# Second layer of a four-layer graph network: turning the rows by copies in SBUF and a block transpose instead of on the tensor engine, with reordered handovers

## The chip, the cores and the metric

One NeuronCore of a Trainium2 chip. The metric is the device time of one execution in microseconds. Three runs of the kernel before gave 2652.57, 2657.73 and 2658.16 us, so the median is 2657.73 us. Engine names are those of the profile: PE is TensorE, PEld its weight load, DVE is VectorE, ACT is ScalarE, POOL is GpSimd, SP is SyncE, which only issues DMAs here.

## What is computed

128 graphs of 64 nodes with 384 features pass four graph layers; each is followed by a residual sum and a layer norm. The change is in the second (`L1_gnn`), which itself has two turns with weights of their own:

```python
temper = float(np.sqrt(H))
adj = adjacency_matrix
adj_tri = jnp.triu(adj, k=1)
diag_mask = jnp.triu(adj, k=0) - adj_tri
h = hidden_state
for l in range(L):                       # L = 2
    m_left = jnp.einsum('bsh,oh->bso', h, W_left[l])
    m_right = jnp.einsum('bsh,oh->bso', h, W_right[l])
    u_left = jnp.einsum('bih,bjh->bij', h, m_left) / temper
    u_right = jnp.einsum('bih,bjh->bij', h, m_right) / temper
    u = u_left * adj_tri + u_left * diag_mask + u_right * jnp.swapaxes(adj_tri, 1, 2)
    delta_exp_u = jnp.exp(u) * adj
    attention = delta_exp_u / (jnp.sum(delta_exp_u, axis=2, keepdims=True) + 1e-10)
    h_lin = jnp.einsum('bsh,oh->bso', h, W_lin[l]) + b_lin[l]
    ctx = jnp.matmul(attention, h_lin)
    h = jax.nn.relu(_layer_norm(ctx, ln_a[l], ln_b[l]))
# around it: x = _layernorm(x + h)
```

## The kernel before

The rows (graph, node) are cut into 16 groups of 512. Three programs follow one another on the same engines: `first_pass` (the first layer, until about 800 us), `rows_pass` (the second, until about 1575 us) and `heads_pass` (third and fourth). They hand over through Python generators: at each `next(after)` of one program, the following one puts a stretch of its own instructions into that engine's queue. The order of every queue is thus written out by hand. All waits are on semaphores, and each engine works its queue strictly in order.

`rows_pass` has 32 slots, four for each of 8 pairs of groups (a, b). Slot 0 is the first turn of group a, slot 1 the first turn of b, slot 2 the second turn of a and slot 3 the second turn of b. A slot on PE is: `projections` (54 matmuls, left and right), `values` 0 and 1, on slots 1 and 2 the 12 `transposes` for the next slot, `pair_scores`, `values` 2 and 3, `context`. A product is made of three of fp32r parts, so the input of a slot is needed with features on the partitions, as a high part (`hhi`, DVE `high_parts`) and a low part (`hlo`, POOL `low_parts`).

How this input comes about differs by turn. In the first turn (`from_x(n)`, slots 0 and 1) SP loads the rows in four strips of 32 features blocks (`load_strips`, tile `blocks`), and DVE turns them by one block transpose (`rows_turned`). In the second turn (slots 2 and 3) ACT writes the normalised context of the slot two before into `z` (`apply`, semaphore `z0_done`), POOL applies gain and shift in eight operations (`z_done`), PE transposes (`t_done`), ACT takes the rectified result out of PSUM into `hf` (`chunks`, `f_done`), and DVE and POOL split it.

DVE's order in a slot: (next slot from strips: `rows_turned`, `high_parts`), `final_sum` and `final_stats` of a finished group, `values_out` 0 and 1 (PE's `values` 2 waits for the first), `final_shift`, (next slot turned: `high_parts`), `one_side` (the masked scores, for which ACT's exponential waits), `values_out` 2, `deltas` (`l_dt`, for which `context` waits), `values_out` 3, `normalise`. ACT's order: `projections_out` 0 and 1, `apply` of the slot before, `projections_out` 2 to 5, `chunks`, `final_apply`, the exponential, `context_out`.

Of the kernel before, what the change touches and what calls it, by code (L numbers as in the profile page):

```python
# [9 lines left out]
ALU = mybir.AluOpType  # L10
# [74 lines left out]
def rows_pass(nc, sh, ctx, groups, first_weight, x_in, strips_in, x_out, adj_d, adjt_d, vec_d):  # L85
# [27 lines left out]
    def entered(n):  # L113

        return 2 * (n // 4) + min(n % 4, 1) + 1
# [32 lines left out]
    x1, x2 = sb("x1", [P, T, D]), sb("x2", [P, T, D])  # L148
# [20 lines left out]
    faggr = sb("faggr", [P, T, 2])  # L169
    sh.rows_stop_at = nc.sbuf_base  # L170
# [17 lines left out]
    t_done = sem("t_done")  # L188
# [33 lines left out]
    def sync_program(sync, after):  # L222
# [22 lines left out]

        first = rows.first
# [24 lines left out]
        sync.wait_ge(first.stored[0], 32)  # L271
        for half in range(2):
            load_x(2, half)
        sync.wait_ge(first.z_done, T * groups)
        load_vectors(1)
        yield
        load_weights(sh, sync, 11, 15)

        for n in range(4 * iters):
            for m, g, half in halves(n):  # L280
                if g + XBUFS < groups:
                    sync.wait_ge(x_used if half else x_half, g + 1)
                    load_x(g + XBUFS, half)
            for g in finished(n):
                store(g)
# [8 lines left out]
            if n + 3 >= 4 * iters and n % 2:  # L294
                next(after)
# [4 lines left out]
    def tensor_program(pe, after):  # L300
        def transposes(n):
            pe.wait_ge(z_done, T * (n - 1))
            for c in range(KC):
                pe.wait_ge(ml_evac, 2 * KC * (n - 1) + (5, 6, 3)[c])
                for t in range(T):
                    mm = nc.tensor.transpose(ring[c][:, t * P:(t + 1) * P], z[n % 2][:, t, c * P:(c + 1) * P],
                                             sh.ident[:, :])
                mm.then_inc(t_done, 1)

# [15 lines left out]
        def projections(n, w0):  # L325
            pe.wait_ge(hi_done, KC * (n + 1))
            for k in range(2 * KC):
# [3 lines left out]
                elif k == 3:  # L331
                    pe.wait_ge(c_evac, T * n)
                elif n and from_x(n):
                    pe.wait_ge(ml_evac, 2 * KC * (n - 1) + (5, 6, 3)[k])
# [8 lines left out]
        def pair_scores(n):  # L343
# [3 lines left out]
            for t in range(T):  # L347
                for c in range(KC):
                    for b in range(2):
                        for half in range(2):  # L350
                            g, first = 2 * t + b, S * b + Q * half
                            keys = blocks[n % 2][:, 2 * g + half, c, :] if from_x(n) else \
                                hf[n % 2][:, c, g * S + Q * half:g * S + Q * half + Q]
                            mm = nc.tensor.matmul(  # L354
                                scores[first:first + Q, t * P + Q * half:t * P + Q * half + 3 * Q],
                                keys,
# [17 lines left out]
        for n in range(4 * iters):  # L374
# [8 lines left out]
            if not last:  # L383
                if not from_x(n + 1):
                    transposes(n + 1)
            else:
# [7 lines left out]
    def scalar_program(act, after):  # L394
        def chunks(n):
            for c in range(KC):
                act.wait_ge(t_done, KC * turned(n) + c + 1)
                act.wait_ge(u_done, max(n - 1, 0))
                act.wait_ge(lo_done, max(KC * (n - 2) + c + 1, 0))
                nc.scalar.activation(hf[n % 2][:, c, :], ring[c][:, :], ACT.Relu)\  # L400
                    .then_inc(f_done, 1)
# [15 lines left out]
        def apply(n):  # L417
            a = n % 2
            act.wait_ge(ab_done, n + 1)
            if n % 4 < 2:  # L420
                act.wait_ge(stored[a], 16 * (n // 4))
            for t in range(T):
# [15 lines left out]
        for n in range(4 * iters):  # L438
            if n:
# [17 lines left out]
        for g in finished(4 * iters - 1):  # L457
            final_apply(g)
# [5 lines left out]
    def vector_program(dve, after):  # L464
# [5 lines left out]
        def rows_turned(n):  # L470
            dve.wait_ge(strips_loaded[n % 2], 16 * STRIPS * (n // 4 + 1))
            nc.vector.transpose(blocks[n % 2][:, :, :, :], blocks[n % 2][:, :, :, :]).then_inc(xt_done, 1)

        def high_parts(n):
            for c in range(KC):
                dve.wait_ge(v_done, max(NPROJ * (n - 1), 0))
                if from_x(n):
                    dve.wait_ge(xt_done, entered(n))
                    nc.vector.tensor_copy(hhi[n % 2][:, c, :].rearrange("p (b r) -> p b r", r=SQ),
                                          blocks[n % 2][:, :, c, :]).then_inc(hi_done, 1)  # L480
                else:
                    dve.wait_ge(f_done, KC * turned(n) + c + 1)
                    nc.vector.tensor_copy(hhi[n % 2][:, c, :], hf[n % 2][:, c, :]).then_inc(hi_done, 1)
# [43 lines left out]
        def final_sum(n, g, half):  # L527
            a = g % 2
            dve.wait_ge(x_loaded[g % XBUFS], 32 * (g // XBUFS) + 16 * (half + 1))
            for t in range(2 * half, 2 * half + 2):  # L530
                dve.wait_ge(z_done, T * n + t + 1)
# [29 lines left out]
        dve.wait_ge(cleared, 2)  # L561
        dve.wait_ge(vec_in[0], 16 * nvec)
        for n in range(4 * iters):
# [9 lines left out]
            for g in finished(n):  # L573
                final_stats(g)
            values_out(n, l, range(0, 2))
# [20 lines left out]
    def gpsimd_program(pool):  # L596
# [3 lines left out]
        def low_parts(n):  # L600
            for c in range(KC):
                pool.wait_ge(hi_done, KC * n + c + 1)
                pool.wait_ge(v_done, max(NPROJ * (n - 1), 0))
                if from_x(n):
                    upper, lower = (part[n % 2][:, c, :].rearrange("p (b r) -> p b r", r=SQ) for part in (hhi, hlo))
                    nc.gpsimd.tensor_tensor(lower, blocks[n % 2][:, :, c, :], upper, ALU.subtract).then_inc(lo_done, 1)
                else:
                    nc.gpsimd.tensor_tensor(hlo[n % 2][:, c, :], hf[n % 2][:, c, :], hhi[n % 2][:, c, :],
                                            ALU.subtract).then_inc(lo_done, 1)
# [19 lines left out]
        yield  # L629
        pool.wait_ge(vec_in[0], 16 * nvec)  # L630
        for n in range(4 * iters):
# [3 lines left out]
            masks(n)  # L635
# [3 lines left out]
            if n + 1 < 4 * iters:  # L639
# [3 lines left out]
            for t in range(T):  # L643
# [10 lines left out]
def first_pass(nc, sh, ctx, groups, xt_in, x_in, x_out, adjt_d, vec_d, row_d, col_d):  # L654
# [49 lines left out]
    rowvec = [sb("rowvec0", [P, D])]  # L704
    sb = placed(sh.at_x0)
# [26 lines left out]
    x_loaded = sem("x_loaded")  # L732
    adj_loaded = [sem(f"adj_loaded{a}") for a in "ab"]
# [35 lines left out]
    first.u_done, first.lo_done = u_done, lo_done  # L769
    first.c_done, first.c_evac, first.z_done, first.stored = c_done, c_evac, z_done, stored  # L770

    def sync_program(sync, after):
# [56 lines left out]
        store(groups - 3)  # L829
        next(after)  # L830
        sync.wait_ge(x_used, groups - 1)
# [1254 lines left out]
```

## Time and profile before

| | us |
|---|---|
| median of 3 runs | 2657.73 |
| the profiled execution | 2652.64 |
| its span, first to last instruction | 2650.9 |
| PE busy in the span | 2570.5 |
| DVE busy | 1998.3 |
| POOL busy | 1521.1 |
| ACT busy | 1219.6 |

The profiled execution is 1.7 us longer than its span. A row of the timeline reads: start, duration, engine, line, operation, output<-input, shape, how many merged, and in brackets the idle time before it with what ended it. A row of a waiting engine at a place is of use only together with what that engine does before and after it, since the queues are in order. The granted clock is 1.00 at TensorE's upper level (2.4 GHz) and 0.50 at the lower (1.2 GHz).

### The profile page before, as it was taken

How to read it: one execution, taken by the hardware profiler on the slowest of the kernel's cores; microseconds unless marked ns; L12 is line 12 of the kernel's file. 1: busy time of each engine (PE TensorE's matmuls, PEld its weight loads, DVE VectorE, ACT ScalarE, POOL GpSimd, SP SyncE). 2: the span in 40 equal slices, each digit the busy share in tenths (PEclk: the TensorE clock that was granted, in tenths of full speed). 3: DMA queues.
4: the chain of work that ended last, by engine and by line, in shares of the span. 5: the costliest groups of instructions: out<-in, count | busy, mean ns of one | idle time of the engine just before them, and what ended most of it. 6: DMA issues, size and time to landing. Idle time of an engine off the chain costs nothing.

```text
span 2650.9 us, 59174 instructions
## 1 busy us (share of the span) xinstructions
PE 2570.5 (97%) x23040; PEld 2237.4 (84%) x23040; DVE 1998.3 (75%) x4485; ACT 1219.6 (46%) x2385; POOL 1521.1 (57%) x1380
## 2 busy tenths in 40 slices
PE   8999999999997999999999997999999999999997
PEld 7998998998986788888888876888888888888886
DVE  5788888888886657666756757888888877777775
ACT  2344444344343344344444443554555555556554
POOL 7657656756757666666667654443444345555553
PEclk9999999999998999999999998999999999999998
DMA  5112112111125122122221224222233223323432
GB/s 162 33 42 70 56 43 69 56 54 58 52 73 155 43 67 73 48 63 67 67 60 53 59 56 108 63 59 71 77 77 77 69 59 87 92 77 89 102 77 75
DMA packets 253286, 187.99 MB, mean 71 GB/s; under 512 B 175568, under 2 KB 250960, under 8 KB 253008
## 3 DMA queue, kind: packets, MB, share of 16 engines
q1 hardware_dynamic: 253008, 184.21, 25.5%
q8 instruction: 184, 3.01, 0.5%
q14 instruction: 94, 0.77, 0.1%
HBM read 133.84 MB, written 50.33 MB: 69 GB/s over the span
## 4 chain that ended last, share of the span: by engine, by line
PE 85%; DVE 5%; POOL 4%; issue 3%; ACT 2%; DMA 1%; SPq 1%; POOLq 0%; ACTq 0%; DVEq 0%
PE bank L1413 14%; PE bank L864 11%; PE bank L1421 11%; PE bank L339 11%; PE pair L864 11%; PE bank L1473 4%; PE pair L1442 4%; PE bank L1459 3%; PE bank L321 2%; PE pair L321 2%; PE bank L850 2%; PE bank L888 2%; PE pair L888 2%; PE bank L354 1%; PE bank L369 1%
## 5 line engine op out<-in xcount | busy, mean ns | idle before, releaser
L1854 POOL TENSOR_TENSOR h_logits<-h_logits,h_mx 128x512 f32<-128x512 f32 x192 | 202.0, 1053 | 267.7 <-DVE h_mx L1697 267.7
L1709 DVE TENSOR_TENSOR h_val<-bank,h_rowvec 64x192 f32<-64x192 f32 x512 | 181.7, 355 | 33.3 <-PE bank L1421 24.2
L407 ACT ACTIVATE l_sides<-bank 128x512 f32<-128x512 f32 x192 | 114.2, 595 | 193.4 <-PE bank L339 193.4
L1150 POOL TENSOR_TENSOR l_hlo<-l_hf,l_hhi 128x576 fp32r<-128x576 f32 x96 | 134.7, 1432 | 115.2 <-ACT l_hhi L981 115.2
L1413 PE MATMUL bank<-h_hhia,whi 128*128 128x512 f32 x450 | 185.3, 412 | 3.3 <-DVE h_hloa L1680 2.3
L1413 PE MATMUL bank<-h_hhia,wlo 128*128 128x512 f32 x450 | 176.7, 393 | 0.0
L1573 ACT ACTIVATE h_keys<-bank,h_keycol,h_halves 128x512 f32<-128x512 f32 x192 | 138.8, 775 | 81.1 <-PE bank L1413 81.1
L1057 DVE TENSOR_TENSOR l_val<-bank,l_vec 64x384 f32<-64x384 f32 x256 | 142.3, 556 | 40.4 <-PE bank L864 37.4
L1057 DVE TENSOR_TENSOR l_val<-pair,l_vec 64x384 f32<-64x384 f32 x256 | 142.3, 556 | 32.1 <-PE pair L864 28.3
L1189 POOL TENSOR_TENSOR l_vdiag<-l_vdiag,l_vec 128x384 f32<-128x384 f32 x128 | 127.6, 1016 | 66.1 <-ACT l_vdiag L962 66.0
L864 PE MATMUL bank<-whi,l_hhi 128*128 128x384 f32 x576 | 141.4, 353 | 5.8 <-POOL wlo L74 5.8
L1597 ACT ACTIVATE h_probt<-bank 128x384 f32<-128x384 f32 x256 | 111.5, 490 | 68.7 <-PE bank L1459 68.6
L981 ACT ACTIVATE l_hhi<-l_hf 128x576 fp32r<-128x576 f32 x96 | 58.6, 673 | 162.4 <-PE pair L864 159.4
L1697 DVE TENSOR_REDUCE h_mx<-h_logits 128x8 f32<-128x512 f32 x192 | 130.8, 681 | 3.3
L642 POOL TENSOR_TENSOR l_small<-l_small,power 128x4 f32<-128x4 f32 x32 | 32.4, 1012 | 174.0 <-DVE l_small L519 174.0
L864 PE MATMUL pair<-whi,l_hhi 128*128 128x384 f32 x576 | 130.8, 334 | 1.5 <-DVE l_val L1057 1.5
L864 PE MATMUL bank<-wlo,l_hhi 128*128 128x384 f32 x576 | 131.6, 336 | 0.0
L864 PE MATMUL bank<-whi,l_hlo 128*128 128x384 f32 x576 | 131.3, 335 | 0.0
L864 PE MATMUL pair<-whi,l_hlo 128*128 128x384 f32 x576 | 131.0, 334 | 0.0
L864 PE MATMUL pair<-wlo,l_hhi 128*128 128x384 f32 x576 | 130.7, 334 | 0.0
L864 PEld LDWEIGHTS bank<-whi,l_hhi 128*128 128x128 f32 x576 | 97.6, 189 | 30.7 <-issue 18.6
L1442 PE MATMUL pair<-h_keys,h_q 64*64 64x128 f32 x3072 | 107.7, 278 | 14.4 <-DVE h_logits L1689 14.4
(267 smaller groups left out, 7699.4 us busy)
## 6 DMA issues: line engine op xcount, KB each, us to landing
h_strips<-x SPq DMA_DIRECT2D x128, 192.0 KB, 5.1
l_hf<-xt SPq DMA_DIRECT2D x16, 864.0 KB, 4.6
l_x<-x SPq DMA_DIRECT2D x16, 768.0 KB, 4.5
l_x<-x SPq DMA_DIRECT2D x32, 384.0 KB, 3.2
h_za<-x SPq DMA_DIRECT2D x16, 768.0 KB, 4.9
h_zb<-x SPq DMA_DIRECT2D x16, 768.0 KB, 5.0
x<-l_zfa SPq DMA_DIRECT2D x8, 768.0 KB, 3.5
x<-l_zfb SPq DMA_DIRECT2D x8, 768.0 KB, 4.3
```

What stands on the lines that cost most here:

```text
L339: mm = nc.tensor.matmul(ring[k % RING][:, :], ww[:, c, m * P:(m + 1) * P], hh[:, c, :], start=(j == 0), stop=(j == len(terms) - 1))
L864: mm = nc.tensor.matmul(ring[k % RING][:, 0:D], hh[:, c, first:first + P], ww[:, c, :], start=(j == 0), stop=(j == len(terms) - 1))
L1057: ins = nc.vector.tensor_tensor(val[half, (g + b) % GRAPHS, 0:D], ring[k % RING][half, 0:D], bias[half, :], ALU.add)
L1150: nc.gpsimd.tensor_tensor(hlo[:, c, :], hf[:, c, :], hhi[:, c, :], ALU.subtract).then_inc(lo_done, 1)
L1189: nc.gpsimd.tensor_tensor(vdiag[:, t, 0:D], vdiag[:, t, 0:D], vec[n % 4 // 2][1][:, :], ALU.add)\
L1413: mm = nc.tensor.matmul(ring[k % 2][:, :], ww[:, c, m * P:(m + 1) * P], hh, start=(c == 0 and j == 0), stop=(c == KC - 1 and j == 2))
L1421: mm = nc.tensor.matmul(out, lhs, rhs, start=(j == 0), stop=(j == len(terms) - 1))
L1442: mm = nc.tensor.matmul(scores[out, 2 * r:2 * r + 2, t, :], q[heads, c, g * S:(g + 1) * S], keys[heads, c, g, :, :], start=True, stop=True)
L1573: ins = nc.scalar.activation(keys[:, c, :, h, :], ring[1][:, :].rearrange("p (g j) -> p g j", j=S), ACT.Identity, scale=halves[:, h:h + 1] ...
L1697: nc.vector.tensor_reduce(mx[:, c, :, ts], row, AX.X, ALU.max)\
L1709: ins = nc.vector.tensor_tensor(val[S * p:S * p + S, 2 * t + b, :, p, 0:HD], src[rows, :, p, :], bias[rows, :, p, :], ALU.add)
L1854: nc.gpsimd.tensor_tensor(row, row, mx[:, c, :, ts].unsqueeze(3).broadcast_to([P, HP, 2, S]), ALU.subtract).then_inc(sub_done, 1)
```

## The change

In the second turn the rows no longer go through PE. `turn_strips` on SP copies `z` within SBUF into the strip layout of `blocks` with 16 DMAs (4 strips by 4 blocks of 32 partitions, 128 pieces of 384 bytes each); DVE turns them with the block transpose; ACT applies gain, shift and rectifier in place, now with features on the partitions and the two vectors as columns (`colvec`). POOL's gain and shift stay only for the second turn's results. PE's transposes are gone. `final_apply` moves behind `context_out`. At the handover from the first layer, DVE turns and splits slot 1's rows and takes the values of slot 0 out before it finishes the last two groups; the last group's residual has a buffer of its own (`last_x`). At the handover to the third layer, the second set of strips is loaded before masks, vectors and weights, and group 14 is stored after those. Weights and vectors are permuted on input to fit. The core of the diff:

```diff
+        def turn_strips(n):
+            sync.wait_ge(z0_done, T * (n - 1))
+            sync.wait_ge(u_done, n - 1)
+            sync.wait_ge(lo_done, KC * (n - 1))
+            by_tile = blocks[n % 2][:, :, :, :].rearrange("p (t q) c a -> p t q (c a)", t=T)
+            for j in range(STRIPS):
+                for q in range(P // SQ):
+                    sync.dma_start(by_tile[SQ * j:SQ * j + SQ, :, q, :],
+                                   z[n % 2][SQ * q:SQ * q + SQ, :, RUN * j:RUN * j + RUN])\
+                        .then_inc(strips_loaded[n % 2], 16)
...
         for n in range(4 * iters):
+            if n and n + 1 < 4 * iters and not from_x(n + 1):
+                turn_strips(n + 1)
             for m, g, half in halves(n):
...
+            if n + 1 == 4 * iters:
+                next(after)
             for g in finished(n):
                 store(g)
...
-            if not last:
-                if not from_x(n + 1):
-                    transposes(n + 1)
...
         def chunks(n):
+            act.wait_ge(col_in, 32)
+            act.wait_ge(xt_done, n + 1)
             for c in range(KC):
-                act.wait_ge(t_done, KC * turned(n) + c + 1)
-                act.wait_ge(u_done, max(n - 1, 0))
-                act.wait_ge(lo_done, max(KC * (n - 2) + c + 1, 0))
-                nc.scalar.activation(hf[n % 2][:, c, :], ring[c][:, :], ACT.Relu)\
+                part = blocks[n % 2][:, :, c, :]
+                nc.scalar.activation(part, part, ACT.Relu, scale=colvec[:, 0, c:c + 1], bias=colvec[:, 1, c:c + 1])\
                     .then_inc(f_done, 1)
...
-                for g in finished(n):
-                    final_apply(g)
...
             context_out(n)
-        for g in finished(4 * iters - 1):
-            final_apply(g)
+            for g in finished(n):
+                final_apply(g)
...
+        rows_turned(1)
+        high_parts(1)
+        split_weights(sh, dve, "hi", *weights_of_slot(0, 0))
+        yield
         dve.wait_ge(vec_in[0], 16 * nvec)
-        for n in range(4 * iters):
+        values_out(0, 0, range(0, 2))
+        yield
+        one_side(0)
+        values_out(0, 0, [2])
+        deltas(0)
+        values_out(0, 0, [3])
+        yield
+        normalise(0)
+        for n in range(1, 4 * iters):
...
             for g in finished(n):
                 final_stats(g)
+            if n + 1 < 4 * iters and not from_x(n + 1):
+                rows_turned(n + 1)
             values_out(n, l, range(0, 2))
...
-            for t in range(T):
+            for t in range(T if n % 4 >= 2 else 0):
                 pool.wait_ge(z0_done, T * n + t + 1)
...
         variance(passes - 1)
         scale_shift(passes - 1)
-        for g in range(groups - 2, groups):
-            final_sum(g, 0)
-            final_sum(g, 1)
-            final_variance(g)
-            final_shift(g)
+        final_sum(groups - 2, 0)
+        final_sum(groups - 2, 1)
+        final_variance(groups - 2)
+        next(after)
+        final_shift(groups - 2)
+        next(after)
+        final_sum(groups - 1, 0)
+        next(after)
+        final_sum(groups - 1, 1)
+        final_variance(groups - 1)
+        final_shift(groups - 1)
...
         load_strips(0)
         yield
+        sync.wait_ge(rows.v_done, T * last_rows)
+        sync.wait_ge(rows.stored[1], 16)
+        sync.wait_ge(xt_done, 1)
+        load_strips(1)
         sync.wait_ge(rows.d_done, last_rows)
```

## Rows read from the trace of the kernel before

**Rows 1.** The page: PE's busy time, the chain by engine.
```profile
PE 2570.5 (97%) x23040; PEld 2237.4 (84%) x23040; DVE 1998.3 (75%) x4485; ACT 1219.6 (46%) x2385; POOL 1521.1 (57%) x1380
PE 85%; DVE 5%; POOL 4%; issue 3%; ACT 2%; DMA 1%; SPq 1%; POOLq 0%; ACTq 0%; DVEq 0%
```

**Rows 2.** Timeline of PE, slots 1, 2, 3 of a middle iteration.
```profile
start us, us, engine line op out<-in xcount [idle before <-releaser]
1219.91 0.53 PE L369 MATMUL bank<-l_val,l_dt 64*64 64x385 f32 x1 [0.93 <-DVE l_dt L505]
...
1221.37 0.96 PE L339 MATMUL bank<-l_hhib,whi 128*128 128x512 f32 x3
...
1236.89 1.47 PE L306 MATMUL bank<-ident,l_za 128*128 128x128 f32 x12
1238.30 2.19 PE L354 MATMUL bank<-l_sides,l_blocksb 128*32 128x96 f32 x96
...
1243.97 0.53 PE L369 MATMUL bank<-l_val,l_dt 64*64 64x385 f32 x1 [0.16 <-DVE l_dt L505]
...
1245.42 0.96 PE L339 MATMUL bank<-l_hhia,whi 128*128 128x512 f32 x3
...
1269.34 0.96 PE L339 MATMUL bank<-l_hhib,whi 128*128 128x512 f32 x3
...
1291.93 0.96 PE L339 MATMUL bank<-l_hhia,whi 128*128 128x512 f32 x3
```

**Rows 3.** Timeline of ACT, slot 1: apply, final_apply, exponential.
```profile
1226.55 2.51 ACT L423 ACTIVATE l_za<-l_craw,l_small 128x384 f32<-128x384 f32 x4 [0.16 <-DVE l_small L525]
...
1238.97 2.51 ACT L429 ACTIVATE l_zb<-l_zb,l_small 128x384 f32<-128x384 f32 x4
```

**Rows 4.** Timeline of DVE: values_out 0, high_parts, and a block transpose.
```profile
1235.53 0.56 DVE L489 TENSOR_TENSOR l_val<-bank,l_vec 128x384 f32<-128x384 f32 x1 [2.30 <-PE bank L321]
...
1238.85 2.19 DVE L483 CAST l_hhia<-l_hfa 128x512 fp32r<-128x512 f32 x3
...
1276.30 1.78 DVE L472 STREAM_TRANSPOSE l_blocksa<-l_blocksa 128x1536 f32<-128x1536 f32 x1 [1.88 <-DMA l_blocksa<-x]
```

**Rows 5.** Timeline of SP's DMA issues: four strips, half a residual.
```profile
1292.77 2.12 SPq L243 DMA_DIRECT2D l_blocksb<-x  x4
1306.15 0.38 SPq L225 DMA_DIRECT2D l_x<-x  x1
```

**Rows 6.** Adjacency issues by source line; DMA view, median from issue to landing.
```profile
L231 SPq DMA_DIRECT2D l_adjna<-adj x32: 616/617/1356, 799.2 to 1505.1; - x32
...
x<-l_za SPq DMA_DIRECT2D x8, 768.0 KB, 3.7
...
l_adjtb<-adjt SPq DMA_DIRECT2D x32, 64.0 KB, 2.3
```

**Rows 7.** First iteration: PE idle in its slot 1, granted clock behind it.
```profile
861.25 0.53 PE L369 MATMUL bank<-l_val,l_dt 64*64 64x385 f32 x1 [3.24 <-DVE l_dt L505]
...
862.70:866.40 3.70, 3.70 (x13) 2.90 (x10) 3.06 (x13) 1.14 (x3) 0.37 (x1) 0.55 0.34 74
```

**Rows 8.** Handover from the first layer: timelines of DVE and PE.
```profile
810.10 0.50 DVE L1094 TENSOR_SCALAR l_small<-l_faggr 128x4 f32<-128x4 f32 x1
815.46 0.16 DVE L1098 SCALAR_TENSOR_TENSOR l_small<-l_faggr,l_small 128x4 f32<-128x4 f32 x1 [4.85 <-POOL l_small L1194]
...
828.73 1.30 PE L321 MATMUL bank<-whi,l_hhia 128*128 128x384 f32 x3 [12.67 <-DVE l_val L489]
```

**Rows 9.** Handover to the third layer: timelines of SP, DVE and PE.
```profile
1573.71 1.77 DVE L1674 STREAM_TRANSPOSE h_xta<-h_strips 128x1536 f32<-128x1536 f32 x1
...
1587.09 0.29 DVE L1779 MEMSET h_val<- 64x48 f32 x2
1587.80 4.72 SPq L1347 DMA_DIRECT2D h_strips<-x  x4
...
1598.93 1.78 DVE L1674 STREAM_TRANSPOSE h_xtb<-h_strips 128x1536 f32<-128x1536 f32 x1 [11.55 <-issue]
...
1605.58 1.99 PE L1442 MATMUL pair<-h_keys,h_q 64*64 64x128 f32 x32 [10.09 <-DVE h_logits L1689]
```

More of the change, by code:

```diff
@@ L111, in finished, with pieces @@
         return [g for m, g, half in halves(n) if half]
-    def entered(n):
-        return 2 * (n // 4) + min(n % 4, 1) + 1
+    def pieces(n):
+        return 4 * STRIPS * (n // 4 + (not from_x(n))) + STRIPS * (n // 4 + 1)
     def turned(n):
@@ L271, in sync_program @@
         sync.wait_ge(first.stored[0], 32)
+        sync.wait_ge(first.x_used, groups)
         for half in range(2):
@@ L275, in sync_program @@
         load_vectors(1)
+        for k in range(2):
+            sync.dma_start(colvec[:, k, :], col_d[k], allow_slow_non_contiguous=True).then_inc(col_in, 16)
         yield
@@ L293, in sync_program @@
                     load_strips(n + 2)
-            if n + 3 >= 4 * iters and n % 2:
+            if n + 3 == 4 * iters:
                 next(after)
@@ L382, in tensor_program @@
             values(n, SLOT[w0 + 2], range(0, 2))
-            if not last:
-                if not from_x(n + 1):
-                    transposes(n + 1)
-            else:
+            if last:
                 for c in range(KC):
@@ L421, in apply @@
                 act.wait_ge(stored[a], 16 * (n // 4))
+            else:
+                act.wait_ge(xt_done, n + 1)
             for t in range(T):
@@ L603, in low_parts @@
                 pool.wait_ge(v_done, max(NPROJ * (n - 1), 0))
[L604 to L609, printed above, removed]
+                upper, lower = (part[n % 2][:, c, :].rearrange("p (b r) -> p b r", r=SQ) for part in (hhi, hlo))
+                nc.gpsimd.tensor_tensor(lower, blocks[n % 2][:, :, c, :], upper, ALU.subtract).then_inc(lo_done, 1)
         def side(out, adjacency, k):
@@ L629, in gpsimd_program @@
         yield
+        masks(0)
+        low_parts(1)
+        yield
         pool.wait_ge(vec_in[0], 16 * nvec)
@@ L634, in gpsimd_program @@
                 pool.wait_ge(vec_in[1], 16 * nvec)
-            masks(n)
+            if n:
+                masks(n)
             for g in finished(n):
@@ L1220, in gpsimd_program @@
         final_power(groups - 2)
+        next(after)
         final_power(groups - 1)
@@ L1374, in sync_program @@
         load_weights(sh, sync, 15, 17)
-        sync.wait_ge(rows.v_done, T * last_rows)
-        sync.wait_ge(rows.stored[1], 16)
-        sync.wait_ge(xt_done, 1)
-        load_strips(1)
         load_adj(1)
@@ L2061, in arrays @@
         if name.startswith("L1_gnn_W"):
-            turn = v[0][strip_order()]
-            v = np.stack([turn if name.endswith("lin") else turn[:, strip_order()], v[1]])
+            v = v[:, strip_order()]
+            v = np.ascontiguousarray(v if name.endswith("lin") else v[:, :, strip_order()])
         out[name] = v.reshape(1) if v.ndim == 0 else v
@@ L2066, in arrays @@
     out["xt"] = np.ascontiguousarray(np.concatenate([xt, xt[..., 0:S]], -1))
+    for m in ("ln_a", "ln_b"):
+        out[f"turned_{m}"] = np.ascontiguousarray(out[f"L1_gnn_{m}"][0][strip_order()])
     out["adjt"] = np.ascontiguousarray(np.swapaxes(out["adj"], 1, 2))
```

59 lines of the change are left out of this document (31 added, 28 removed).

## The prediction, made before the changed kernel was run

> **What bounds the kernel now.** I read the page first. PE is busy 97% of the span and makes 85% of the chain that ended last [rows 1], so only what shortens PE's queue, or what makes PE wait, moves the time. Next I read the timeline of PE over one middle iteration of the second layer, because an average says nothing about a single slot. From one projection start to the next, slot 1 takes 24.05 us (1221.37 to 1245.42), slot 2 takes 23.92 and slot 3, which has no transposes, 22.59 [rows 2]. PE waits 0.93 us for `l_dt` at the end of slot 0 and 0.16 us at the end of slot 1. So in the middle of the layer PE is the bound, and DVE's delivery of `l_dt` comes nearly last. Third, the timelines of the two handovers: there PE waits, 12.67 us for DVE's `values_out` [rows 8] and 10.09 us for DVE's first logits [rows 9].
>
> **What leaves PE.** Twelve transposes per turned slot, from 1236.89 to 1238.30, are 1.41 us [rows 2]; 16 turned slots make 22.6 us. All of it is on the path today. It is a gain only if the new way delivers in time, so the rest of the working is about that.
>
> **When the new way delivers.** I count from the start S of slot 1 or 2. Its steps:
> 1. `apply` of the slot before ends at 1229.06, S+7.7 [rows 3]. SP's wait ends there.
> 2. SP issues 16 DMAs. No SBUF-to-SBUF DMA is in the trace. The nearest issue is that of the strips, also 384-byte pieces onto 32 partitions: four in 2.12 us, 0.53 each [rows 5]. From below, a residual load costs 0.38 [rows 5]; from above, an adjacency load 0.62 [rows 6]. I take 0.53, and the last issue then starts 15 x 0.53 = 8.0 us after the first. The ends are 5.7 and 9.3.
> 3. The last one lands. The smallest frequent DMA, 64 KB, takes a median of 2.3 us from issue [rows 6]; these carry 48 KB. I take 2.3 and allow 0.5 either way. The landing L in slot 2 is thus S + 7.7 + 0.1 + 8.0 + 2.3 = S+18.1.
> 4. DVE's block transpose takes 1.78 us [rows 4]. It stands ahead of `values_out` 0 in DVE's queue, which takes 0.56 [rows 4] and for which PE's `values` 2 waits. PE resumes at L+2.4 or so. Without the transposes PE has finished the scores at S + (1238.30 - 1221.37 - 1.41) + 2.1 = S+17.6.
> 5. Behind it stand `values_out` 1, then `high_parts`. ACT's three affine operations run beside them, the same in number as the evacuations they replace. From the start of `high_parts` to `context` the trace shows 1238.85 to 1243.97, 5.1 us, with nothing waiting in between; from `context` to the next projection 1.45 us [rows 2, 4]. `high_parts` starts at L+3.0, `context` at L+8.1, and the next slot at L+9.6.
>
> The cycle of slot 2 becomes 18.1 + 9.6 = 27.7 us against 23.92, 3.8 us more.
>
> In slot 1, `apply` writes a `z` tile that must be stored first. The store now waits for `final_apply` behind `context_out` of slot 0, which ends at about S+1.1: plus 2.51 [rows 3] and a store of 3.7 us [rows 6], `apply` starts near S+7.5 and ends at S+10.0. Then L is S+20.4 and the cycle 30.0 us against 24.05, 6.0 us more. SP's other waits in these slots (masks, store) are over by S+6.7 and hide nothing else: the residual loads pushed behind the turn have three buffers.
>
> The DMA page of the Trainium skill (DMA: Bandwidth & Descriptors, section Anatomy of one DMA) puts one DMA at about 2.0 us fixed plus its bytes at 436 GB/s. By it, 48 KB would land 2.1 us after issue instead of 2.3; over 16 turns that is an estimated 3 us less, which does not change the verdict.
>
> **What PE's clock adds.** After an idle time of 3.24 us in the first iteration the granted clock is 0.55 over the next 3.7 us, mostly the 1.2 GHz level [rows 7]. The new idle time ahead of `values` 2 is L + 2.4 - 17.6, so 2.9 us in slot 2 and 5.2 in slot 1. PE has 2.4 us of slack between `values` 3 and `context`, since DVE's chain is later, and most of a slow stretch falls there. I take 0.5 us per slot, with bounds of 0 and 2.
>
> **The rest of the slots.** In slot 0 the exponential no longer stands behind `final_apply`; the 0.93 us wait for `l_dt` shrinks by about 0.7, eight times, 5.6 us. POOL's eight gain and shift operations in slots 1 and 2 cost nothing today and their removal gives nothing, because they end ahead of the transposes. Masks and low parts have more room.
>
> **Handovers.** From the first layer: DVE is through with group 14's variance at 810.6 [rows 8]. Then come the transpose (1.78) and three copies (2.19) [rows 4], stretched by POOL's work beside them, and a weight split, some 7.5 us together; `final_shift`, which POOL releases at 815.46 [rows 8], is covered by them. So `values_out` 0 ends near 818.7, and today PE resumes behind it at 828.73. PE resumes 10 us earlier. But group 15's store now ends later than the first context (an estimate: its second half is summed behind `values_out` 3 near 825, then statistics, POOL's power, 2.51 us of `final_apply` and 3.7 us of store, so 835). Slot 1's `apply` waits for it and ends near 837.7, and the turn waits for `apply`. By the steps above (10.4 to the landing, 9.6 behind it) slot 2 starts at 857.7 instead of 861.25 + 1.45 = 862.7 [rows 7]. Slot 2 then costs some 2 us less than today, as today's has an idle time like the one of [rows 7] as well. Of the 10 us, 7 stay for the whole first iteration.
>
> To the third layer: DVE waits until 1598.93 for strips issued at 1587.80, behind ten other DMAs; it was free at 1587.4 [rows 9]. The first strips are turned by 1573.71 + 1.77 = 1575.5 [rows 9]; issued then, the second ones have landed when DVE is free. DVE and PE's first logits come 11 us earlier. I take 11, with 8 and 20 (if the slow clock behind the idle time goes too) as bounds.
>
> **The sum.** Seven iterations of 6.0 + 3.8 = 9.8 are 68.6; the clock 14 x 0.5 = 7.0; slot 0 gives back 5.6, the first iteration 7, the last handover 11. Together +52 us on the profiled execution's 2652.6, so 2705. The median run is 5 us above that execution and I put the forecast at 2707.
>
> **Rivals.** (a) *The turn is hidden.* If the 16 DMAs are issued and landed by about S+14, DVE's transpose waits for nothing and each turned slot takes 22.6 us. Then the whole 22.6 us comes back, slot 0 gives 5.6, and the handovers 10 + 11: about 2603. It decides at 6.5 us from `apply` to landing; against it stands that even issues of 0.38 us make 5.7 + 2.3 + 0.1 = 8.1, and slot 1 has 2.3 us more to lose. I give everything faster than before 12%. (b) *Short issues.* At 0.38 us the turn is 2.3 us shorter in each of 14 slots: 2675. (c) *Long issues and a slow clock.* At 0.62 us and 2 us of clock per slot: 14 x (1.3 + 1.5) = 39 more, 2746; if the DMAs also back up in the rings, as the four strips of 4.72 us do [rows 9], over 2780. (d) *The turn only breaks even* with shorter issues and a larger handover gain: 2650 to 2662.
>
> **How the numbers follow.** My case (2685 to 2730) has 45%, (b) 17%, (c) 20%, (d) 6%, (a) and what lies near it 12%. The range is 2660 to 2780; it leaves out (a) and (d) and the end of (c). A measurement of this kernel can tell about 0.2%, 5 us, from no change. Faster by more than that 0.12, within 0.05, slower 0.83.
>
> **What would show it.** Right: in slots 1 and 2 PE idles about 3 to 5 us ahead of `values` 2, ended by DVE's `values_out`, and 1 to 2.5 us ahead of `context`; DVE idles ahead of its transpose until the turn's DMA lands near S+18 and S+20; the cycles of slots 1 and 2 are near 30 and 28 us, those of slots 3 and 0 unchanged; PE's logits at the last handover come 11 us sooner after the last context. Wrong: DVE's transposes waiting for nothing, or issues well below 0.4 us each. The whole forecast hangs on the time from `apply` to landing: each microsecond of it is worth 14 to 16 us.

## The result, and the profile after

| | before | after |
|---|---|---|
| median | 2657.11 us | 2762.37 us (2760.41 to 2764.16) |
| the profiled execution | 2652.6 us, span 2650.9 | 2761.3 us, span 2759.5 |
| PE busy | 2570.5 us, 97% | 2574.8 us, 93% |

The ratio is 1.0405 (95% interval 1.0392 to 1.0418). The change costs 105 us; the forecast was 50. The direction and the main mechanism, a turn that lands too late, held; the size was off by about two. The median before is here of four runs.

The page of the kernel after, busy times and chain by engine and by line:

```profile
PE 2574.8 (93%) x22848; PEld 2241.3 (81%) x22848; DVE 2027.0 (73%) x4501; ACT 1225.3 (44%) x2385; POOL 1388.2 (50%) x1252
...
PE 70%; DVE 6%; SPq 6%; issue 5%; DMA 4%; ACT 4%; POOL 4%; DVEq 0%; POOLq 0%; ACTq 0%
```

SP's queue is now 6% of the chain, where it was 1%, and PE's share fell from 85% to 70% [rows 1]. PE is not less busy in microseconds, although 192 transposes are gone: other matmuls ran at a lower clock, as the window below shows.

Slot 2 of a middle iteration, from the timelines of PE, ACT, SP and DVE of the kernel after (start and length in us, engine, line, operation; in brackets the idle time before it and what ended it):

```profile
1200.18 0.96 PE L351 MATMUL bank<-l_hhia,whi 128*128 128x512 f32 x3
1207.51 2.51 ACT L432 ACTIVATE l_zb<-l_craw,l_small 128x384 f32<-128x384 f32 x4 [2.32 <-DMA x<-l_zb]
1210.04 11.04 SPq L256 DMA_DIRECT2D l_blocksb<-l_zb  x16
1222.58 1.78 DVE L481 STREAM_TRANSPOSE l_blocksb<-l_blocksb 128x1536 f32<-128x1536 f32 x1 [16.44 <-DMA l_blocksb<-l_zb]
1224.95 1.30 PE L333 MATMUL bank<-whi,l_hhia 128*128 128x384 f32 x3 [6.97 <-DVE l_val L497]
...
1229.68 0.94 DVE L513 TENSOR_TENSOR l_dt<-l_e,l_adjta 128x256 f32<-128x256 f32 x1
...
1232.47 0.96 PE L351 MATMUL bank<-l_hhib,whi 128*128 128x512 f32 x3
```

The slot takes 32.29 us (1200.18 to 1232.47) against 23.92 [rows 2]. `apply` waits 2.32 us for a store and ends at S+9.8; SP issues 16 transfers in 11.04 us; they have landed at 1222.58, S+22.4, 12.5 us after `apply`; DVE sat idle for 16.44 us and PE for 6.97. The next slot begins 9.9 us after the landing. The next slot 1, from 1278.56, has the same shape: 32.28 us, PE idle 6.92 us. Over the 14 turned slots behind the first iteration the landing comes 12.4 us after `apply` on the mean (11.7 to 13.0), and the next slot 9.6 us after the landing (9.55 to 9.92). The seven iterations behind the first average 110.2 us, against 94.5 before.

PE's clock behind that idle time, one row of the window view (busy times of PE, PEld, DVE, ACT, POOL, granted clock, DMA share, GB/s):

```profile
1224.90:1231.50 6.60, 6.55 (x26) 5.82 (x26) 5.74 (x9) 2.19 (x4) 4.10 (x3) 0.55 0.00 0
```

A granted clock of 0.55 is mostly the 1.2 GHz level. `values` 2 and 3 take 6.1 us instead of 3.4.

The same kernel's first iteration, SP, ACT and PE:

```profile
837.17 2.51 ACT L432 ACTIVATE l_za<-l_craw,l_small 128x384 f32<-128x384 f32 x4 [3.11 <-DVE l_small L533]
...
844.10 0.37 SPq L82 DMA_DIRECT2D stage<-L_gnn_Wk  x1
847.41 0.37 SPq L82 DMA_DIRECT2D stage<-L_gnn_Wv  x1
847.87 0.60 SPq L234 DMA_DIRECT2D l_adjta<-adjt  x1
...
850.56 10.36 SPq L256 DMA_DIRECT2D l_blocksa<-l_za  x16
864.67 1.30 PE L333 MATMUL bank<-whi,l_hhib 128*128 128x384 f32 x3 [19.90 <-DVE l_val L497]
```

`apply` ended at 839.7, 2.0 us behind the forecast, and what it waited for last was DVE's scale and shift, some 0.4 us behind the store. But the turn was issued only at 850.6. SP stood in `load_weights`: each load waits until an earlier weight has been split, and those loads stand ahead of the loop. Slot 1 took 45.88 us.

The handover to the third layer, PE, SP and DVE of the kernel after:

```profile
1696.69 0.47 PE L1450 MATMUL bank<-h_hhia,whi 128*128 128x512 f32 x1 [2.29 <-DVE h_hloa L1717]
...
1707.08 1.78 DVE L1711 STREAM_TRANSPOSE h_xtb<-h_strips 128x1536 f32<-128x1536 f32 x1
...
1715.09 1.10 PE L1479 MATMUL pair<-h_keys,h_q 64*64 64x128 f32 x32
```

DVE's second block transpose no longer waits (before: 11.55 us), and PE no longer idles for 10.09 us [rows 9]. The third layer's first projection starts 119.7 us later than before, at 1696.69 instead of 1577.01, while the span grew by 108.6: the handover gives back 11.1 us.

### The profile page after: what moved, and what is told of

Same layout as the page of the kernel before. It is cut to its first block, busy times and chain, and to the rows that moved or that the text cites. A ratio compares the mean times of both kernels' runs of the same rounds, so it can differ in the third digit from the quotient of the medians.

```text
span 2759.5 us, 58937 instructions
## 1 busy us (share of the span) xinstructions
PE 2574.8 (93%) x22848; PEld 2241.3 (81%) x22848; DVE 2027.0 (73%) x4501; ACT 1225.3 (44%) x2385; POOL 1388.2 (50%) x1252
## 4 chain that ended last, share of the span: by engine, by line
PE 70%; DVE 6%; SPq 6%; issue 5%; DMA 4%; ACT 4%; POOL 4%; DVEq 0%; POOLq 0%; ACTq 0%
PE bank L1450 14%; PE bank L1458 11%; PE bank L889 11%; PE pair L889 10%; SPq L256 5%; PE bank L351 4%; PE pair L1479 4%; PE bank L1510 4%; PE bank L1496 3%; PE bank L875 2%; PE bank L913 1%; PE pair L913 1%; PE bank L333 1%; DMA x<-l_za 1%; PE pair L333 1%
## 5 line engine op out<-in xcount | busy, mean ns | idle before, releaser
L627 POOL TENSOR_TENSOR l_hlob<-l_blocksb,l_hhib 128x512 fp32r<-128x512 f32 x48 | 65.1, 1377 | 154.5 <-DVE l_hhib L490 154.5
L481 DVE STREAM_TRANSPOSE l_blocksb<-l_blocksb 128x1536 f32<-128x1536 f32 x16 | 28.5, 1779 | 143.4 <-DMA l_blocksb<-l_zb 128.9
L627 POOL TENSOR_TENSOR l_hloa<-l_blocksa,l_hhia 128x512 fp32r<-128x512 f32 x48 | 64.9, 1374 | 118.6 <-DVE l_hhia L490 118.6
```

## The experiments

Ratios are to the kernel before, run on the same chip. Slots are measured from one projection start to the next.

**The handovers alone (h1).** The kernel before, with nothing but the reordered handovers:

```diff
 # the kernel before; transposes, column chunks and final_apply stay
+        rows_turned(1); high_parts(1)      # DVE, ahead of groups 14 and 15 of the first layer
+        values_out(0, 0, range(0, 2))
...
+        load_strips(1)                     # third layer, ahead of adjacency, vectors and weights
```

> The kernel before with only the reordered handovers (first to second layer, second to third); the transposes stay on PE. Theory (the second turn's new way alone makes the loss, the handovers gain): the last handover gives 10.3 us, as in the trace after (second scores start 18.4 us behind the first projection of the third layer instead of 28.6). Of the first, 9.2 us show at the start of slot 1, but slot 1's transposes then wait for gain and shift on GpSimd (end near 848), and 3 us stay: 13 us less than before, ratio 0.995, some 2640 us. Rival: all 19.5 us stay, ratio 0.993. Rival: the handovers give nothing by themselves, ratio 1.000.

Measured: 2639.98 us, ratio 0.9938 (0.9922 to 0.9955). The handovers gain 16 us, so the rest of the change, the turn with `final_apply`'s new place and SP's order, costs 122 us over 16 slots, 7.7 us each. In the first handover PE resumed 10 us sooner, but most of it was lost one slot on (ACT and PE of h1):

```profile
837.09 2.52 ACT L428 ACTIVATE l_za<-l_craw,l_small 128x384 f32<-128x384 f32 x4 [2.67 <-DMA x<-l_zfb]
...
847.22 2.82 PE L311 MATMUL bank<-ident,l_za 128*128 128x128 f32 x12 [4.23 <-POOL l_za L669]
```

`apply` waits for the first layer's last store and PE's transposes wait 4.23 us for POOL behind it. Slot 1 takes 34.3 us instead of 27.5, and the first iteration is 3.4 us shorter, not 10.

**Half of the transfers from ACT's queue (q1).**

```diff
+            apply(n - 1)
+            turn_strips(act, n + 1, range(2, 4))   # ACT: strips 2 and 3
...
-            turn_strips(n + 1)
+            turn_strips(sync, n + 1, range(0, 2))  # SP: strips 0 and 1
```

> The changed kernel with 8 of the 16 DMAs of each turn issued by ScalarE's queue behind apply, the other 8 by SyncE. Theory (the turn is bound by the issues, 0.69 us each one after another on one queue): the last landing comes 5.5 us earlier, each turned slot is some 5.5 us shorter, 16 times 5.5 makes 88 us less than the changed kernel: 2674 us. Rival (the issues of two queues slow each other, the engines behind them are the limit): issues take 1.2 us each on both queues and the time stays within 10 us of 2762. Rival (ScalarE's evacuations behind its issues come late and TensorE waits for them): between, 2700 to 2740, with a wait of TensorE for l_sides.

Measured: 2678.99 us, ratio 1.0088 (1.0068 to 1.0108). Timelines of ACT, both queues and DVE in q1, slot 1 of a middle iteration:

```profile
1149.56 2.51 ACT L432 ACTIVATE l_za<-l_craw,l_small 128x384 f32<-128x384 f32 x4 [2.37 <-DMA x<-l_za]
...
1152.10 5.20 ACTq L232 DMA_DIRECT2D l_blocksa<-l_za  x8
1152.10 5.79 SPq L232 DMA_DIRECT2D l_blocksa<-l_za  x8
...
1159.43 1.78 DVE L483 STREAM_TRANSPOSE l_blocksa<-l_blocksa 128x1536 f32<-128x1536 f32 x1 [6.31 <-DMA l_blocksa<-l_za]
```

Two queues issue side by side at the same pace as one, 0.65 and 0.72 us each. The landing comes 7.4 us after `apply` here and 7.1 on the mean, instead of 12.4, and 83 us come back: issuing is what made the turn long. The Trainium skill (DMA: Bandwidth & Descriptors, section Issuing engines are not separate DMA queues) says that starting DMAs on several engines saves only the time to initiate them, usually small relative to the DMA. The first half agrees with this run. The second holds for a single transfer, 0.7 us of issue against a median of 2.0 from issue to landing. It does not hold for 16 in a row: their landings overlap and their issues do not, so the issues took 11.0 us and the last landing 2.0.

**final_apply ahead of the exponential again (f1).**

```diff
+                for g in finished(n):
+                    final_apply(g)
             act.wait_ge(mx_done, n + 1)
             # exponential
             context_out(n)
-            for g in finished(n):
-                final_apply(g)
```

> The changed kernel with final_apply ahead of the exponential again, as in the kernel before. Theory (in slots 1 and 2 apply waits 2.3 us for the store of the group finished one slot earlier, and the turn for apply): both turns land some 2.2 us earlier, 15 times, 33 us less than the changed kernel: 2729 us. The wait of apply for the store is gone in slots 1 and 2. Rival (the exponential now waits 2.5 us for final_apply and context comes that much later): no gain or up to 20 us more.

Measured: 2745.01 us, ratio 1.0337 (1.0316 to 1.0357): 17 us gained, about half of what was expected. ACT in f1, slot 2 of a middle iteration (S = 1195.97):

```profile
1201.97 2.51 ACT L432 ACTIVATE l_zb<-l_craw,l_small 128x384 f32<-128x384 f32 x4 [0.98 <-DVE l_small L535]
```

The store's wait is gone, but `apply` then waits for DVE's scale and shift, and ends at S+8.5 instead of S+9.8. A removed wait is worth only the distance to the next one. Slot 0 loses a little again: PE waits 1.08 us for `l_dt` on the mean, against 0.73 in the changed kernel.

**The block transpose behind values 0 and 1 (o1).**

```diff
-            if n + 1 < 4 * iters and not from_x(n + 1):
-                rows_turned(n + 1)
             values_out(n, l, range(0, 2))
             for g in finished(n):
                 final_shift(g)
+            if n + 1 < 4 * iters and not from_x(n + 1):
+                rows_turned(n + 1)
```

> The changed kernel with VectorE's block transpose of the second turn behind values_out 0 and 1 instead of ahead of them; nothing else. TensorE's values 2 and 3 then wait for nothing. Theory (the slot's end hangs on the landing of the turn, since the masked scores stand behind the split in VectorE's queue): only the 1.0 us of values_out leaves the path, 16 times, 10 to 16 us less than the changed kernel: 2746 to 2752 us; the wait of TensorE moves to context (some 9 us) and may keep the clock low in the next slot's start. Rival (the wait ahead of values 2 is itself the loss): 6.9 us less per turned slot, about 2655 us.

Measured: 2784.95 us, ratio 1.0487 (1.0466 to 1.0508), 22 us slower than the changed kernel, where some 10 to 16 us of gain were expected. PE and DVE in o1, slot 2 (S = 1212.52), and a window at its end:

```profile
1234.84 1.78 DVE L481 STREAM_TRANSPOSE l_blocksb<-l_blocksb 128x1536 f32<-128x1536 f32 x1 [6.03 <-DMA l_blocksb<-l_zb]
...
1237.62 0.43 DVE L490 CAST l_hhib<-l_blocksb 128x512 fp32r<-128x512 f32 x1 [1.01 <-ACT l_blocksb L407]
...
1242.88 0.90 PE L379 MATMUL bank<-l_val,l_dt 64*64 64x385 f32 x1 [9.21 <-DVE l_dt L513]
...
1245.65 1.39 PE L351 MATMUL bank<-l_hhib,whi 128*128 128x512 f32 x3
...
1243.00:1247.00 4.00, 4.00 (x20) 1.80 (x21) 2.00 (x5) 1.75 (x4) 0.00 (x0) 0.55 0.30 69
```

The landing is still at S+22.3. `values` 2 and 3 no longer wait, so PE's idle time moves from ahead of them to ahead of `context`: 9.21 us. The low clock follows it there, onto matmuls that are on the path: from `context` to the next projection 2.8 us, against 1.45 before [rows 2]. The 1.0 us of `values_out` brings nothing on DVE either: the first high copy now waits 1.01 us for ACT's affine operation, which `values_out` had covered. The next slot begins 10.8 us after the landing in all 14 slots, against a mean of 9.6 in the changed kernel.

**Weights 13 and 14 behind the first turn (w1).**

```diff
-        load_weights(sh, sync, 11, 15)
+        load_weights(sh, sync, 11, 13)
...
                 turn_strips(n + 1)
+                if n == 1:
+                    load_weights(sh, sync, 13, 15)
```

> One change to the changed kernel: SP issues the loads of weights 13 and 14 behind the first turn's 16 transfers, no longer ahead of the loop, where they wait for slot 1's weight split and hold the turn back. Theory (the queue's order made the first iteration long): apply ends at 839.7 and the turn was issued only at 850.6, so it moves up by about 10.7 us, slot 1 of the first iteration shrinks from 45.9 to 35.2 us and nothing else moves: 2752 us, ratio to the kernel before 1.036. Rival (in that slot the residual load, the weight split or the late adjacency is the next to be late): 2 to 4 us gained, 2759 us, with PE still idle for more than 15 us ahead of the scores' end.

Measured: 2753.26 us, ratio 1.0377 (1.0361 to 1.0392): 9 us gained, where 10 were expected. ACT, SP and PE in w1, first iteration:

```profile
838.73 2.51 ACT L434 ACTIVATE l_za<-l_craw,l_small 128x384 f32<-128x384 f32 x4 [3.12 <-DVE l_small L535]
...
841.93 11.30 SPq L256 DMA_DIRECT2D l_blocksa<-l_za  x16
853.28 0.59 SPq L82 DMA_DIRECT2D stage<-L_gnn_Wk  x1
...
857.02 1.30 PE L335 MATMUL bank<-whi,l_hhib 128*128 128x384 f32 x3 [11.57 <-DVE l_val L499]
```

SP issues the turn 0.7 us behind `apply` and the weights after it. PE idles 11.57 us instead of 19.90, and slot 1 takes 37.3 us instead of 45.9.

**The turn by way of DRAM (d1).**

```diff
-            for j in range(STRIPS):
-                for q in range(P // SQ):
-                    # 16 transfers within SBUF, 48 KB each
+            sync.dma_start(x_out[group(n)], z[n % 2][:, :, :]).then_inc(spilled[n % 2], 16)
+            sync.wait_ge(spilled[n % 2], 16 * (n // 4 + 1))
+            # four strip loads, as in load_strips
```

> The turn goes by way of DRAM: one store of z to the group's rows (128 pieces of 6 KB) and four strip loads as those of the first turn, in place of the 16 transfers within SBUF. Theory (the turn is long by its 16 issues, 11.0 us, and not by moving bytes): from the end of apply 0.2 us, landing of the store 3.7, 0.2 to the next issue, three of four issues 1.6, landing of the last strip 3.8: 9.5 us against 13.2. Each of 16 turned slots is 3.5 us shorter, 2762 - 56 = 2706 us; with PE's stall a little shorter the clock gives back 0 to 10 more: 2696 to 2712, ratio 1.017 to 1.021. Rival (the pieces' size or the DMA engines' work made it long): two landings in a row, each over 768 KB, cost as much as the 16 issues: 2760 us.

Measured: 2719.26 us, ratio 1.0246 (1.0231 to 1.0262). ACT, SP and DVE in d1, slot 1:

```profile
1158.45 2.51 ACT L432 ACTIVATE l_za<-l_craw,l_small 128x384 f32<-128x384 f32 x4 [2.45 <-DMA x<-l_za]
...
1160.99 0.36 SPq L254 DMA_DIRECT2D x<-l_za  x1
1164.54 2.88 SPq L257 DMA_DIRECT2D l_blocksa<-x  x4
...
1170.85 1.78 DVE L481 STREAM_TRANSPOSE l_blocksa<-l_blocksa 128x1536 f32<-128x1536 f32 x1 [8.96 <-DMA l_blocksa<-x]
```

Out to DRAM and back takes 9.9 us from the end of `apply` here and 9.6 on the mean, 2.8 less than 16 short transfers within SBUF; over 16 turns that is 45 us, and 43 were measured. I had expected 56, from 13.2 us for the old way (it is 12.4) and 9.5 for the new.

**Three edits together (b0)**: the edits of q1, f1 and w1 in one kernel.

```diff
+                    turn_strips(act, n + 1, range(2, 4))   # q1
+                for g in finished(n): final_apply(g)       # f1, ahead of the exponential
+                    load_weights(sh, sync, 13, 15)         # w1, behind the first turn
```

> Three single edits together: half of the turn's transfers issued by ACT's queue, final_apply ahead of the exponential again, weights 13 and 14 loaded behind the first turn. Theory (each takes its own piece of the path from the end of apply to the landing, and they add): 2762 - 83 - 17 - 10 = 2652 us, ratio 0.998. A typical iteration 23.2 + 25 + 25 + 22.6 = 96 us. Rival (with the landing at 16 us behind the slot's start the slot's end hangs on DVE's sequence block transpose, values, high copies, products, exponential and delta, and the landing no longer counts): final_apply's place brings nothing, 2669 us.

Measured: 2655.42 us, ratio 1.0006 (0.9996 to 1.0015). One by one the three gained 83, 17 and 9 us, together 107: they add, and the change as a whole is then worth nothing.

**DVE's order in a turned slot (b1, b2).** Both start from b0. b2 moves only the high copies; b1 moves the final shift and `final_apply` too:

```diff
+            if to_turn: final_shift(g); rows_turned(n + 1)     # b1; b2 leaves final_shift where it was
             values_out(n, l, range(0, 2))
-                    high_parts(n + 1)
+                    high_parts(n + 1, [0])
             one_side(n)
             values_out(n, l, [2])
             deltas(n)
             values_out(n, l, [3])
+                high_parts(n + 1, [1, 2])
```

> As the three edits together, and DVE's order in a turned slot changed: the final shift ahead of the block transpose, then values 0 and 1, high copy 0, the two score products, values 2, deltas, values 3, and high copies 1 and 2 last; final_apply ahead of the column scaling. Theory (behind the landing the slot's end hangs on DVE's queue: high copies of 2.3 us stand ahead of the products): up to 2 us less in each of 16 turned slots than with the three edits alone, turned slots 23.3 to 24.0 us, iteration 92.5 to 94, 2632 us (2620 to 2642), ratio 0.991. Rival (the scores on PE or the high copies moved behind now hold the next slot's first projection): turned slots 25 us, 2652 us or more.

> The kernel of the three edits together, with one thing of the fastest variant: high copies 1 and 2 behind values 3. Final shift and final_apply stay as in the three edits. Theory (of the 31 us between the two, the high copies' place carries most, as they stood 2.1 us ahead of the score products): 2655 - 24 = 2631 us, 2626 to 2638, ratio 0.991. Rival (it was final_apply's and the final shift's place): 2650 us.

Measured: b1 2624.24 us, ratio 0.9889 (0.9872 to 0.9905); b2 2629.53 us, ratio 0.9901 (0.9886 to 0.9916). b2 has 26 of the 31 us, so the copies' place carried most. DVE and PE in b1, slot 2 (S = 1137.88):

```profile
1153.42 1.78 DVE L487 STREAM_TRANSPOSE l_blocksb<-l_blocksb 128x1536 f32<-128x1536 f32 x1 [9.58 <-DMA l_blocksb<-l_zb]
...
1156.00 0.79 PE L335 MATMUL bank<-whi,l_hhia 128*128 128x384 f32 x3
...
1158.77 0.43 DVE L519 TENSOR_TENSOR l_dt<-l_e,l_adjta 128x256 f32<-128x256 f32 x1
...
1160.87 0.96 PE L353 MATMUL bank<-l_hhib,whi 128*128 128x512 f32 x3
```

With the landing at S+15.5, `values` 2 waits for nothing, and the slot takes 22.99 us: in slot 2 PE is the bound again and the removed transposes are a gain. In slot 1 PE mostly still waits 0.6 to 1.0 us for `l_dt`. b1 is the fastest kernel of the study, 16 us ahead of h1; their intervals don't touch. In the profiles 10 of these come in the first iteration (103.8 us against 113.8, most of it in its slot 2) and only 6 in the seven others (93.7 us each against 94.6).

**What the low clock costs (c1, a1, c2).** In c1 and c2 PE repeats the 96 score matmuls where it would idle (same operands, same result); a1 is the changed kernel with b1's order on DVE and ACT but all transfers on SP, and c2 is a1 with the repeats:

```diff
-            for t in range(T):
+            for t in list(range(T)) * (4 if n % 4 in (1, 2) else 1):   # c1; 3 in c2
```

> The changed kernel with PE kept busy where it waited: in slots 1 and 2 the 96 score matmuls are done four times over (same operands, same result, 6.5 us more work on PE), in the 7 us in which PE idled ahead of values 2. Theory (the low clock behind the idle time falls into PE's slack, since deltas on DVE end only 1 us before context): values 2 and 3 take 3.3 instead of 6.0 us, but the slot is 0 to 1 us shorter: 2762 - 8 = 2754 us, 2746 to 2762, ratio 1.037. Rival (the clock is what the slots lost): 2.8 us a slot, 2717 us or less. Below 2762 by nothing, or above it, would mean that the added matmuls delay values 2.

> The changed kernel with the queue order of the fastest variant on DVE and ACT (final shift ahead of the block transpose, high copies 1 and 2 behind values 3, final_apply ahead of the column scaling), but all 16 transfers on SP and SP's order as in the changed kernel. Against the variant with only final_apply moved (2745 us) it differs behind the landing alone. Theory (with PE idle 5.5 us, values 2 and 3 at the low clock take 5 to 6 us and now end last, so DVE's shorter order finds PE slow): the order brings 0.3 us a slot, 2740 us, ratio 1.032. Rival (the order is worth as much as with both queues issuing, 31 us or 1.9 a slot): 2714 us, ratio 1.022.

> As the run with the new DVE and ACT order and 16 transfers on SP, and the score matmuls of slots 1 and 2 done three times over, so that PE's idle time ahead of values 2 is 1 us in place of 5.4. Theory (in that run PE's low clock holds the slot): values 2 and 3 at the full clock take 3.3 us, context comes 1.5 to 2 us sooner in each of 16 slots: 2712 us (2706 to 2720), ratio 1.021. Rival (DVE's path from landing to delta holds it in either case): no change from the run without the repeats, within 5 us.

Measured: c1 2785.63 us, ratio 1.0491 (1.0475 to 1.0507); a1 2743.36, 1.0327 (1.0312 to 1.0343); c2 2727.43, 1.0275 (1.0258 to 1.0292). Landing, `values` 2 and next slot in a1, then in c2:

```profile
1187.30 1.78 DVE L483 STREAM_TRANSPOSE l_blocksa<-l_blocksa 128x1536 f32<-128x1536 f32 x1 [9.04 <-DMA l_blocksa<-l_za]
1189.66 1.30 PE L333 MATMUL bank<-whi,l_hhib 128*128 128x384 f32 x3 [5.90 <-DVE l_val L499]
...
1195.84 0.96 PE L351 MATMUL bank<-l_hhia,whi 128*128 128x512 f32 x3
```

```profile
1181.25 1.78 DVE L483 STREAM_TRANSPOSE l_blocksa<-l_blocksa 128x1536 f32<-128x1536 f32 x1 [9.65 <-DMA l_blocksa<-l_za]
1183.61 0.76 PE L333 MATMUL bank<-whi,l_hhib 128*128 128x384 f32 x3 [1.98 <-DVE l_val L499]
...
1188.54 0.96 PE L351 MATMUL bank<-l_hhia,whi 128*128 128x512 f32 x3
```

From the landing to the next slot: 8.54 us in a1, 7.29 in c2. These two slots make the difference small: over the 14 turned slots behind the first iteration the means are 9.2 and 7.4. That 1.8 us a slot is the price of the low clock where DVE's order is short. b1's order by itself brings nothing clear as long as SP issues all transfers: a1 has 2743.36 us and f1 2745.01. c2 gained 16 us over a1, half of what I expected; its landings come 0.4 us later on the mean. In c1, where DVE's long order stays, the same stretch is:

```profile
1199.02 1.78 DVE L481 STREAM_TRANSPOSE l_blocksa<-l_blocksa 128x1536 f32<-128x1536 f32 x1 [12.31 <-DMA l_blocksa<-l_za]
...
1201.39 0.76 PE L333 MATMUL bank<-whi,l_hhib 128*128 128x384 f32 x3 [0.67 <-DVE l_val L497]
...
1207.11 0.53 PE L379 MATMUL bank<-l_val,l_dt 64*64 64x385 f32 x1 [2.35 <-DVE l_dt L513]
...
1208.56 0.98 PE L351 MATMUL bank<-l_hhia,whi 128*128 128x512 f32 x3
```

9.54 us, though `values` 2 and 3 ran at the full clock. The changed kernel, at the low clock, takes 9.55 to 9.57 in 11 of 14 slots and 9.70 to 9.92 in three; the slot shown first is the second longest of them. So behind DVE's long order the clock costs nothing in most slots and at most 0.35 us: it makes `values` 2 and 3 2.7 us longer, and PE has 2.35 us to spare ahead of `context` in c1. As a whole c1 was 23 us slower, the wrong way for either theory. The landing comes 13.3 us after `apply` here (ended at 1185.72) and 14.0 on the mean, against 12.4, which is 21 us over 14 slots. In six of the 14 slots the stretch behind the landing is longer too, 9.9 to 10.9 us; at 1318.93 `context` itself runs at a granted clock of 0.50 behind 2.32 us of idle time. Why transfers land later while PE repeats matmuls was not tested. The page of c1 shows more instruction traffic by DMA, 218 packets against 182, but no run ties it to the landings. So c1 bounds the clock's term, and the cause of its later landings stays open.

## Why the prediction was off by half

Between the two profiled executions 108.6 us were added; the sum had 52. They are made of +109.6 in seven iterations (forecast 71), +10.0 in the first (forecast -7) and -11.1 at the last handover (forecast -11).

- **Landing, step 2: mis-sized.** This is the term that failed most. Sixteen issues take 11.04 us, 0.69 each, and 10.3 to 11.6 in the 16 turns; I took 0.53 from four strip loads [rows 5]. My upper end was 0.62, from adjacency loads [rows 6]. The median issue is 0.60 us long, inside that bound. But they start 0.64 us apart, since a gap stands between them, and in 11 of the 16 turns one issue takes 1.0 to 1.8 us; what makes an issue that long was not tested. The sum for 16 thus lay outside the bounds. Landing was shorter, 2.0 us instead of 2.3. From `apply` to landing it was 12.4 us on the mean, not 10.4: 2.0 us, 14 times, 28 us. q1 and d1 show that this is what the time hangs on. The section of the Trainium skill that the forecast names beside this step (DMA: Bandwidth & Descriptors, section Anatomy of one DMA) is on DMAs issued by GpSimd, and these are issued by SP; its 2.1 us from issue to landing is near the 2.0 all the same.
- **apply in slot 2: a step left out.** I let `final_apply`'s new place delay `apply` in slot 1 and took slot 2's from the kernel before, S+7.7. But the odd group's store stands in slot 2's way in the same manner (ACT idles 2.32 us for it): S+9.8, 2.1 us, 7 times, 15 us. f1 removes this wait. In slot 1 the step was right (forecast S+10.0, measured S+9.9).
- **First iteration: a queue not walked.** I had `apply`'s end 2.0 us early (837.7 against 839.7) and put it down to the store, where DVE's scale and shift came last, some 0.4 us behind it. Then I wrote that the turn waits for `apply`. It waited for SP, which stood in weight loads that wait for splits. Instead of a gain of 7 us there is a loss of 10. w1 recovers 9 of these 17 by order alone. In w1 the landing still comes 13.4 us after `apply` instead of 10.4, and slot 2 takes 30.9 us, where I let it cost 2 us less than the 29.5 of before.
- **Slot 0: wrong limiter.** The wait for `l_dt` shrank by 0.3 us and not by 0.7: 0.73 on the mean of seven slots against 1.05. The exponential no longer stands behind `final_apply`, but then waits for DVE's masked scores (7.41 us of idle time on ACT, ended by `l_ut`, ahead of the exponential at 1165.55). Three microseconds.
- **Behind the landing: right.** PE resumes 2.37 us after the landing (forecast 2.4) and the next slot starts at 9.6 on the mean and 9.9 in the slot shown (forecast 9.6 and 0.5 for the clock). PE's idle times of 6.97 and 6.92 us replace 2.9 and 5.2 only because the landing is later.
- **The clock: too high.** The forecast set down 0.5 us a slot, 7 us. The stretch behind the landing is 9.6 us with the low clock, as it was forecast without it, and c1 leaves at most 0.35 us and mostly nothing. The reason given, PE's slack ahead of `context`, was right.
- **Handovers.** `values_out` 0 was forecast to end near 818.7, and PE resumed behind it at 818.37; the last handover, forecast at 11 us, was 11.1.

Over the seven iterations the excess of 39 us is thus 28 from the landing, 15 from slot 2's `apply` and 3 from slot 0, less 7 for the clock that cost next to nothing. One slip of the sum does not matter here: 2705 and 5 us make 2710, not 2707.

Of the rivals, (c), long issues, came nearest (2746), in part by luck: 21 of its 39 us are a slow clock that did not come. The range of 2660 to 2780 held, but its upper part rested on that clock and on transfers backing up, not on slot 2's `apply` or the first iteration.

## What to carry to other kernels

When a change moves data with many small DMAs, cost the issues first: here 16 of them took 11 us and landing 2. Price them by a row of the same source and destination or leave the upper end wide open, and walk the issuing queue item by item in the first iteration too, since it starts differently. What removes work from the bound engine gains nothing until the new path delivers inside that engine's own work; splitting the issues over two queues, moving `final_apply` and two weight loads, and putting first on the consumer's queue what the bound engine waits for turned +4.0% into -1.1%. The handovers alone (h1) give 0.6 of these 1.1. And read a term from all slots, not from one: one slot made the clock's price 0.35 and 1.25 us, where all of them make it near nothing and 1.8.

## What the runs showed of the hardware

- Issues of 48 KB transfers within SBUF take 0.69 us each on one queue (11.04 us for 16; the median issue is 0.60 us long, about as long as that of an adjacency load from DRAM, 0.62); from two queues at once 0.65 and 0.72 each, side by side. The Trainium skill (DMA: Bandwidth & Descriptors, section Anatomy of one DMA) has descriptor generation as small and says that many descriptors can be emitted before its cost shows. That section is on DMAs issued by GpSimd; these are issued by SP and ACT, so no run here tests it.
- These transfers land in a median of 2.0 us, and a 768 KB store in 3.7. DMA view of the kernel after (count, size of one, median us to landing):

```profile
l_blocksa<-l_za SPq DMA_DIRECT2D x128, 48.0 KB, 2.0
...
x<-l_za SPq DMA_DIRECT2D x8, 768.0 KB, 3.7
```

- Where PE's idle time stands decides what its low clock costs: 0 to 0.35 us ahead of work with slack (the changed kernel and c1), 1.8 us a slot where `values` end last (a1 and c2), and 1.2 us a slot when the same idle time moved ahead of `context` (o1, 22 us in all).
- The delta product on DVE takes 0.94 us with POOL's low parts beside it (1229.68, above) and 0.43 us without them (b1, 1158.77). The Trainium skill (GPSIMD Engine Reference, section Specifications) says that POOL's SBUF interface is shared with VectorE and that they contend when a DVE instruction has two SBUF inputs; this trace agrees.
